# A sparse-attention layer with sorted experts: GpSimd's order, a projection in two halves, the first tiles and the pads

## What is computed

```python
def layer(x, adj):                       # cut from the reference
    n = layernorm(x)
    q, k, v = n @ Wq.T + bq, n @ Wk.T + bk, n @ Wv.T + bv      # 4 heads of 32
    scores = clip(q @ k.T / sqrt(32), -10, 10); scores = where(mask == 0, -10, scores)
    # softmax over EACH chunk of 128 keys by itself; the 8 chunks' contexts are added
    ctx = sum over chunks of softmax(scores[chunk]) @ v[chunk]
    out = ctx @ Wo.T + bo + n
    x = x + layernorm(out) * gamma + beta
    m = layernorm(x)
    two = top2(m @ Wg + bg)
    return x + sum over e in two of (gelu(m @ W1[e] + b1[e]) @ W2[e] + b2[e])
```

## Time and profile before

| | us |
|---|---|
| median of 3 runs | 852.67 |
| lowest, highest | 850.55, 852.83 |
| the profiled execution | 852.1 |
| its span | 850.5 |
| first clip begins, last clip begins | 38.3, 592.1 |
| first finish of a tile, last | 621.9, 839.1 |

### The profile page before, as it was taken

How to read it: one execution, slowest core, us unless ns; L and a number is a source line. 1 busy time by engine, 2 the same in 40 slices (tenths; PEclk the granted TensorE clock), 3 DMA queues, 4 the chain that set the end, 5 groups by cost and what they waited for, 6 DMA issues and landing times. The chain is left out here.

```text
span 850.5 us, 17280 instructions
## 1 busy us (share of the span) xinstructions
PE 722.9 (85%) x5499; PEld 377.7 (44%) x5499; DVE 626.5 (74%) x1472; ACT 491.2 (58%) x873; POOL 591.9 (70%) x674
## 2 busy tenths in 40 slices
PE   2688998998989989899899898787577879999994
PEld 1222233232333333333323333231277768999994
DVE  2178898898988989889898898989774544455552
ACT  2456666766667666676665765635244535666662
POOL 4697665978779787797886977848764556445553
PEclk9989999999999999999999999998787989999998
DMA  7100000011010110101100001003211246432330
GB/s 260 62 1 25 14 13 13 13 39 50 14 39 13 39 50 13 39 13 39 50 13 26 14 27 37 14 26 110 76 54 57 68 133 189 123 85 85 102 93 1
DMA packets 45255, 45.43 MB, mean 53 GB/s; under 512 B 7413, under 2 KB 39424, under 8 KB 44720
## 3 DMA queue, kind: packets, MB, share of 16 engines
q1 hardware_dynamic: 38800, 30.00, 12.6%
q0 software_dynamic: 6368, 14.34, 4.8%
HBM read 31.46 MB, written 18.34 MB: 59 GB/s over the span
## 5 line engine op out<-in xcount | busy, mean ns | idle before, releaser
L641 ACT ACTIVATE e<-e 128x2048 f32<-128x2048 f32 x128 | 244.3, 1910 | 184.1 <-DVE e L783 181.3
L783 DVE SCALAR_TENSOR_TENSOR e<-scores_ps,bound_mem 128x2048 f32<-128x2048 f32 x128 | 291.9, 2281 | 43.8 <-PE scores_ps L393 42.4
L1189 POOL DMA_INDIRECT out<-e,near x91 | 90.3, 993 | 100.2 <-DVE e L964 51.7
L1167 POOL TENSOR_TENSOR ctx_part<-ctx_part,z_inv 128x1024 f32<-128x1024 f32 x62 | 119.8, 1933 | 49.1 <-DVE z_inv L799 49.1
L706 ACT ACTIVATE e<-scores_ps,bound_mem 128x128 f32<-128x128 f32 x364 | 103.8, 368 | 71.0 <-PE scores_ps L532 55.5
L412 PE MATMUL z_ps<-e,one_column 128*32 128x512 f32 x1024 | 137.4, 609 | 0.0
L1179 POOL TENSOR_TENSOR ctx_sum<-ctx_sum,ctx_part 128x512 f32<-128x512 f32 x90 | 115.8, 1287 | 6.0
L532 PE MATMUL scores_ps<-e,bound_mem 128*128 128x128 f32 x728 | 103.3, 287 | 13.7 <-DVE bound_mem L946 7.6
L532 PEld LDWEIGHTS scores_ps<-e,bound_mem 128*128 128x128 f32 x728 | 93.6, 201 | 17.4 <-issue 11.0
L946 DVE COPY bound_mem<-bound_mem 128x258 f32 x182 | 51.3, 324 | 55.6 <-issue 54.9
L791 DVE STREAM_TRANSPOSE ctx_part<-ctx_ps 128x512 f32<-128x512 f32 x128 | 90.1, 704 | 0.1
(11 more groups left out here) (156 smaller groups left out, 1046.7 us busy)
## 6 DMA issues: line engine op xcount, KB each, us to landing
near<-sorted_rows SPq DMA_DIRECT2D x91, 130.0 KB
near<-in_x SPq DMA_DIRECT2D x16, 256.0 KB
bound_mem<-in_adjT SPq DMA_DIRECT2D x4, 1024.0 KB, 11.0
x_post<-in_x SPq DMA_DIRECT2D x16, 256.0 KB, 2.7
sorted_rows<-sorted_rows SPq DMA_DIRECT2D x16, 130.0 KB
sorted_rows<-sorted_rows POOLq DMA_DIRECT2D x12, 130.0 KB
out<-e,near POOLq DMA_INDIRECT x91
sorted_rows<-x_rows,slot POOLq DMA_INDIRECT x64
```

The costliest lines, as they stand in the source:

```text
L641: nc.scalar.activation(every, every, ACT.Exp, scale=SCORE_SCALE).then_inc(exp_done, 1)
L783: dve.scalar_tensor_tensor(out=e[:, s % E_RING], in0=scores_ps[:], scalar=-CLIP, in1=to, op0=ALU.max, op1=ALU.min).then_inc(clipped, 1)
L1167: nc.gpsimd.tensor_tensor(pair, pair, z_inv[:, v % 2, j:j + 2].to_broadcast([P, 2, SQUARES, DH]), ALU.mult).then_inc(ctx_scaled, 1)
L1189: nc.gpsimd.indirect_dma_start(out=out_rows, out_offset=bass.IndirectOffsetOnAxis(ap=near_u[:, id_at:id_at + 1], axis=0), in_=e_flat[:, at ...
```

## The change

1. *GpSimd's order in a block.* Scale, addition, scale now stand ahead of root 2; two additions and a scale ahead of the residual; two additions and a scale ahead of root 3; then two additions. In the last block the scatter of block 12 moves from the end to behind the first scale.
2. *Projection.* `project` takes a range of token tiles; in blocks before the last, four of its eight matmuls stand in step 1 and four in step 2. The rank moves from step 5 to step 6. ScalarE's normalise of the incoming x moves from step 7 to behind the exponential of the next block's step 0.
3. *Hand-over.* The loops end with the last block; the last two contexts, VectorE's turns, the gate and choice of block 13, the projection of block 14 and the sums of block 15 stand in slots 0 to 2 among the tiles. The router's steps get slots with numbers 3 higher or so; the two scales of block 15 go from slot 0 to slots 3 and 4. The read of a tile's offsets (`load_offsets`) moves behind the copy of the tile ahead.
4. *Pads.* SyncE issues 12, two behind each of loads 28 to 33, GpSimd 10 from slot 22, ScalarE 6 from slot 22, one a slot.

```diff
-SP_PADS = 16
-PAD_LOAD, PAD_SLOT = 19, 21
+SP_PADS, POOL_PADS = range(0, 12), range(12, 22)
+ACT_PADS = range(22, NP)
+PAD_LOAD, PAD_SLOT = 28, 22
...
-                if i >= PAD_LOAD and n_padded < SP_PADS:
-                    pad(n_padded)
-                    n_padded += 1
+                for k in SP_PADS[max(2 * (i - PAD_LOAD), 0):max(2 * (i - PAD_LOAD) + 2, 0)]:
+                    pad(k)
...
-                    if j == (2 if last else 1) and is_block(u - 2):
-                        project(u - 2)
+                    if last and j == 2:
+                        project(13)
+                    if not last and j in (1, 2) and is_block(u - 2):
+                        project(u - 2, range(2 * j - 2, 2 * j))
...
                 if k < FFN_TILES:
                     turn_tile(k)
+                if k < LAG:
+                    context(STEPS - LAG + k)
+                if k == 0:
+                    gate(13)
+                if k == 1:
+                    project(14)
...
+            load_offsets(0)
             for k in range(SLOTS):
+                if k < FFN_TILES:
+                    copy_weights(k)
+                if k + 1 < FFN_TILES:
+                    load_offsets(k + 1)
+                if k < LAG:
+                    turn(STEPS - LAG + k)
                 if k == 0:
-                    scale_last(4)
-                    scale_last(6)
...
+                if k in (3, 4):
+                    scale_last(2 * k - 2)
...
+                if k == PAD_SLOT:
+                    act.wait_ge(pad_at_ready, 1)
+                    act.wait_ge(spare_padded, 16)
+                if 0 <= k - PAD_SLOT < len(ACT_PADS):
+                    pad(ACT_PADS[k - PAD_SLOT])
+                if k == 0:
+                    act.wait_ge(z_added, STEPS - 1)
+                if k == E_RING - 1:
+                    act.wait_ge(z_added, STEPS)
```

More of the change, by code:

```diff
@@ L475, in rank, with project @@
                           skip_group_check=True).then_inc(rank_filled, 1)
-            def project(v):
+            def project(v, tiles=range(TILES)):
                 pe.wait_ge(ctxT_ready, v + 1)
@@ L480, in project @@
                 pe.wait_ge(xnT_bo_ready, v + 1)
-                for t in range(TILES):
+                for t in tiles:
                     cols = slice(t * P, (t + 1) * P)
@@ L484, in project @@
                     ins = pe.matmul(job_ps[1][:, cols], xnT_bo[:, v % 4, cols], ident[:], start=False, stop=True)
-                ins.then_inc(proj_filled, 1)
+                if TILES - 1 in tiles:
+                    ins.then_inc(proj_filled, 1)
             def columns(g):
@@ L564, in _ @@
             pe.matmul(job_ps[1][:, 0:1], w_proj[:, W_O, :], bv_sb[:], start=True, stop=True).then_inc(bias_filled, 1)
-            for u in range(FIRST, BLOCKS + 1):
-                for j in range(CHUNKS if u < BLOCKS else LAG):
+            for u in range(FIRST, BLOCKS):
+                for j in range(CHUNKS):
                     s = u * CHUNKS + j
@@ L587, in _ @@
                         queries(u + 2)
-                    if j == (1 if last else 5) and is_block(u - 3):
+                    if j == (1 if last else 6) and is_block(u - 3):
                         rank(u - 3)
@@ L707, in gelus, with pad @@
                                          bias=part_flat[:, bias_at:bias_at + 1]).then_inc(hidden_ready, 1)
+            def pad(k):
+                at = act.value_load(pad_at[0:1, k:k + 1], min_val=0, max_val=SPARE * P)
+                act.dma_start(sorted_rows[bass.ds(at, P), :], sorted_tiles[SPARE]).then_inc(padded_act, 16)
             act.wait_ge(proj_loaded, 16 * 8)
             act.wait_ge(ident_ready, 1)
-            for u in range(FIRST, BLOCKS + 1):
-                for j in range(CHUNKS if u < BLOCKS else LAG):
+            for u in range(FIRST, BLOCKS):
+                for j in range(CHUNKS):
                     s = u * CHUNKS + j
@@ L715, in _ @@
                         exponentials(s)
+                    if j == 0 and is_block(u + 2):
+                        normalise_x(u + 2)
                     if j == 2 and is_block(u + 2):
@@ L932, in _, with load_offsets @@
             offsets_of = {}
[L934 to L937 removed]
+            def load_offsets(i):
                 if i in GROUP_OF:
@@ L1194, in _ @@
             for u in range(FIRST, BLOCKS):
+                last = u == BLOCKS - 1
                 if is_block(u - 1):
                     scale(u - 1, 0)
+                if last:
+                    scatter(u - 3)
+                if is_block(u - 1):
+                    add_context(u - 1, 1)
+                    scale(u - 1, 2)
                 if is_block(u - 2):
@@ L1199, in _ @@
                 if is_block(u - 1):
-                    add_context(u - 1, 1)
-                    scale(u - 1, 2)
                     add_context(u - 1, 2)
+                    add_context(u - 1, 3)
+                    scale(u - 1, 4)
                 if is_block(u - 2):
@@ L1205, in _ @@
                 if is_block(u - 1):
-                    add_context(u - 1, 3)
-                    scale(u - 1, 4)
                     add_context(u - 1, 4)
+                    add_context(u - 1, 5)
+                    scale(u - 1, 6)
                 if is_block(u - 2):
@@ L1211, in _ @@
                 if is_block(u - 1):
-                    add_context(u - 1, 5)
-                    scale(u - 1, 6)
                     add_context(u - 1, 6)
@@ L1226, in _ @@
                     ins.then_inc(gates_spread, 1)
-                if is_block(u - 3):
+                if is_block(u - 3) and not last:
                     scatter(u - 3)
@@ L1237, in _ @@
             for k in range(SLOTS):
[L1238 removed]
+                if k == 7:
                     root(ln["3"], 14)
[L1240 to L1242 removed]
+                if k in (8, 9):
+                    scatter(13, (2 * k - 16, 2 * k - 15))
+                if k == 10:
                     root(ln["2"], 15)
[L1244 removed]
+                if k == 11:
                     add_residual(15)
[L1246 removed]
+                if k == 14:
                     root(ln["3"], 15)
[L1248 to L1251 removed]
+                if k in (15, 16):
+                    scatter(14, (2 * k - 30, 2 * k - 29))
+                if k in (22, 23):
+                    scatter(15, (2 * k - 44, 2 * k - 43))
                 if k == PAD_SLOT:
@@ L1254, in _ @@
                     pool.wait_ge(spare_padded, 16)
-                if 0 <= k - PAD_SLOT < NP - SP_PADS:
-                    pad(SP_PADS + k - PAD_SLOT)
+                if 0 <= k - PAD_SLOT < len(POOL_PADS):
+                    pad(POOL_PADS[k - PAD_SLOT])
                 if k >= 2:
```

120 lines of the change are left out of this document (54 added, 66 removed).

## The result

The kernel after runs in **818.13 us** (median of 4 runs, 817.23 to 819.39), the kernel before beside it in 852.75. The ratio is 0.9596, 95% interval [0.9568, 0.9623]: 34.6 us faster, against a forecast of 823. The profiled execution of after has a span of 816.4 us and a mean granted clock of 0.972.

A forecast was written before the change was run, and what follows sets the result against it. The prediction took the wait cycle between GpSimd's running sum and VectorE to bound attention, and tile loads and stalls the tiles before tile 32. Blocks −20 and hand-over with pads −9 took 852.1 to 823 us; range 806 to 842.

The forecast's parts named there:

- the ring was the bound: Attention blocks: GpSimd's sum, VectorE's turn of it and z_inv wait for each other in a cycle; 823 us, chance 50%.
- part 1: GpSimd's order in the attention blocks: additions and scales cover the root's wait; 1.2 us a block, 13 blocks, 16 us.
- part 3: Hand-over from attention to tiles: tile 0 finished 12.1 us earlier, 5.4 us given back by VectorE's work between tiles.
- part 2: Projection halved over steps 1 and 2 of a block: saves a 0.85 us wait in about every second block, 4 us.
- The last clip: Sign at the end of attention: the last clip ends near 575 us; later than 585 would be wrong.
- keeps its spacing in slots, and so do its stalls: Block 15's router chain among the tiles: its spacing and stalls in slots stay, so the loss up to tile 32 was left.
- Part 4: Pads among the tile loads: 6 us of load waits gone, 1.5 us added at SyncE and 2 at ScalarE.
- a granted clock of 0.5 in more than 10 us of the tiles: Sign in the tile phase that would show the prediction wrong.
- (d): Tile phase: lower clock level gone from the first 20 tiles and stalls halved; 808 us, chance 10%.
- (e): Tile phase: thin start leaves TensorE idle, at the lower clock through the router's slots; slower, 861 us at 20 slots, chance 6%.
- exclusion: Shared SBUF port between tiles: each VectorE scale could wait for a whole GpSimd scale, 3.8 us more; left out.

The follow-up runs named there:

- after's second run: The kernel after, unchanged, run again on another chip than the first: 811.04 us, ratio 0.9622 to the kernel before.
- the later runs: The kernel after, unchanged, run twice more on chips where before takes 842 us: 811.04 and 812.35 us, ratios 0.9622 and 0.9641.

## Why the prediction was right

The chosen case, "the ring was the bound", holds, and 823 lies 5 us above the result. But the terms behind it are not all of the size forecast, and some luck is in the sum: part 1 gives 6 us or more beyond its term, part 3 gives 4 to 7 us where 6.7 was forecast, with a give-back much larger than its term, and part 2 has its size from another wait than the one it prices.

- **Part 1, forecast 16, measured 22 to 24.** The mechanism is as told: the root's wait is covered, the sum comes earlier, the block falls to 33.0 to 33.2 us (forecast 33.4). The term that was mis-sized is the gain per block, 1.2 us over 13 blocks; it is 1.8. It was capped at 1.5 by the time at which TensorE issued the next block's scores. But TensorE itself waited for VectorE's clips, 20.9 us between 130 and 530 us with the old order and 10.3 in after's second run, so its scores come earlier too, and the cap moves. Another 0.3 was taken off for TensorE's turn of xn2. That give-back isn't there: between 130 and 530 us this wait is 6.0 us in 12 places in after and 5.9 in 12 with the old order.
- **Part 2, forecast 4, measured 2.3 to 4.4: the size by luck.** It prices a wait of 0.85 us for the scores of step 2 in about every second block. In before's trace the wait is in 3 of the 12 blocks from 3 to 14, 2.5 us in all, and each time TensorE was granted the lower clock level (1.2 GHz) for some 3.4 us just ahead of it. These three blocks take 35.7 to 35.9 us, the others 34.8, and the block that was read is one of the three. With GpSimd's new order alone, and with the projection whole again, the wait is in none of these blocks, and the granted clock is 1.00. So this part's wait goes with part 1. What the projection's halves and the rank's move give is the 0.23 us a block seen above. The rows are before, just ahead of its wait in block 8, and the kernel with the whole projection:

```profile
314.00:318.00 4.00, 4.00 (x24) 1.14 (x21) 3.90 (x15) 1.23 (x2) 3.36 (x4) 0.57 0.56 168
```

```profile
38.00:560.00 522.00, 480.15 (x3683) 171.00 (x3683) 476.69 (x904) 341.65 (x368) 429.25 (x421) 1.00 0.09 28
```

- **The last clip**, forecast to end near 575, ends at 570.99, by the error in part 1.
- **Part 3, forecast −12.1 and +5.4, and the step that failed.** The start is as forecast: the wait of 1.3 us for tile 0's load measured 1.38, and tile 0 is finished 13.4 us behind the last clip's end (forecast 15, before 27.5), though 15.4 and 17.1 in the later runs. Some 3.9 of this belong to GpSimd's order in the last block, so of the forecast's net of 6.7 about 3 are left for the hand-over itself; it measured 0 to 3. The term that was mis-sized is the give-back: beside the kernel without the hand-over, tile 0 comes 7 to 9 us sooner behind the last clip, as forecast (12.1 less the 3.9), but 8.3 to 10.1 are given back up to tile 32, not 5.4. What the forecast left out stands in its own sentence, that the chain for block 15 "keeps its spacing in slots, and so do its stalls". The forecast made the stalls a property of the slots. They are one of time: z_inv comes 4.7 us later with tile work ahead of it, the tiles start 8 us sooner, and a shift by 3 slots doesn't make up for both. The rows gave z_inv; following the chain from it to ctxT in time, and the tiles beside it, would have shown the stall at slot 8.
- **Part 4, forecast −2.5, measured −4.0 to −5.6.** The forecast took 15.0 us in 12 places as TensorE's waits for loads. That row adds two queues of one engine that stand at the same time, the weight loads (8.2 us in 7 places) and the matmuls. The matmuls alone waited 6.8 us in 5 places, 3.0 of them for the first two tiles:

```profile
PE scores_ps L521 <- DMA near<-sorted_rows: 6.8, 5, 2.3
```

  So the 6 us that the forecast took as gone were more than the 3.8 there. In after these waits are 1.4 us in the first execution (under 6 forecast), 4.9 and 6.5 in the two later ones, of which 3.5 and 5.0 fall at tiles 31 to 33, where none was forecast up to 32. What ScalarE's six pads cost by themselves wasn't measured, and the term was measured with the hand-over in place; without it, projection and pads together give 2.6 us.
- **The clock.** The lowest rows of 10 us in the tiles are 0.67 (600 to 610) and 0.66 (620 to 630), both at a stall of TensorE of over 4 us. At 0.5 or 1.00, the two levels, a row of 0.67 is 6.6 us at the lower one. From 570 to 700 us the mean is 0.88, so about 31 us of 130 were at the lower level: the sign "a granted clock of 0.5 in more than 10 us of the tiles" was there, and it told nothing, since before has the same 0.88 from 594 to 728. Rivals (d) and (e) did not come about: the low level neither went nor spread.
- **The port.** The prediction left out exclusion, 3.8 us by the rule. Alone, VectorE's scale takes 1.22 us, an addition of tile work 0.29, two copies 0.49 and an addition of the sum 0.69; GpSimd's scale takes 1.92 and its next three instructions 1.3 each. Where they meet, one of the two is longer each time:

```profile
585.56 1.22 DVE L829 TENSOR_TENSOR ctx_part<-ctx_part,z_inv 128x1024 f32<-128x1024 f32 x1 [0.43 <-issue]
585.65 2.90 POOL L1199 TENSOR_TENSOR ctx_part<-ctx_part,z_inv 128x1024 f32<-128x1024 f32 x1
586.70 2.00 DVE L979 TENSOR_TENSOR bound_mem<-near 128x128 f32<-128x128 f32 x1
589.01 1.23 DVE L970 COPY bound_mem<-bound_mem 128x258 f32 x2
590.16 2.29 DVE L829 TENSOR_TENSOR ctx_part<-ctx_part,z_inv 128x1024 f32<-128x1024 f32 x1
591.33 2.24 POOL L1191 TENSOR_TENSOR x_post<-x_post,rows 128x512 f32<-128x512 f32 x1
592.37 1.75 DVE L845 TENSOR_TENSOR ctx_sum<-ctx_part 128x512 f32<-128x512 f32 x1
```

That is what the Trainium skill (SBUF — State Buffer, on the shared port pair) lets expect: the addition has two SBUF inputs and is held for most of a GpSimd instruction. VectorE's four longer rows make 4.6 us between 586 and 594, 3.0 of them beyond what the forecast's 5.4 holds, against the 3.8 that it left out. The later runs of after repeat it (4.6 and 4.4 us). How much of it reaches the time of the kernel isn't shown.

The later runs make a chain of kernels, each by its ratio: GpSimd's order, the last block's included, 26.5 us; projection and pads together 2.6 more; the hand-over 1.1 or 2.7. After measured 31.8 and 30.2 by its two ratios. The terms that were measured by taking one part out of after add up to 32 or more (22 to 24, 2.3 to 3.9, 4.0 to 5.6, and the 3.9 of the last block), so they overlap.

## What to carry to other kernels

Where two engines wait for each other in a ring, look for the wait of one that has work of the other's queued behind it: moving ready work ahead of such waits, 3.2 us of it ahead of a 2.5 us wait and more further on, with nothing made faster, gave most of this gain. Starting a phase earlier gives little if steps of the phase before it are tied to slots of the new one: their data keeps its time, so their slots must move later, or they must stand behind the slot's ready work. And a gain at the start of a phase is only counted once a late instant (here the finish of tile 32 and that of tile 89) has been looked at. Before a wait is priced, read it in every block of the trace, not in one, and look at the clock beside it: the 0.85 us of part 2 stood in 3 blocks of 12. And check whether a row of waits adds two queues of one engine.

## What the runs showed of the hardware

The first chip's traces, of before and of after, have places between 634 and 692 us, and a shorter one at 617, where VectorE or ScalarE stands 2 to 5 us and the profile names no instruction on this core as the releaser ("remote"). TensorE stands for 1 to 3 us beside most of them; GpSimd works on in after's. In after:

```profile
DVE e L988 <- remote: 11.3, 3, 4.9
ACT e L716 <- remote: 7.1, 2, 4.6
```

In before VectorE has 6.5 us of these in 2 places and ScalarE 13.3 in 4. None of the twelve traces of the other chips has one, two of them of the same kernel after, so they belong to the chip or the moment, not to the kernels. They are of the size of the difference between the chips (853 and 842 us for before, 818 and 811 to 812 for after), but not all of it: the 57 tiles behind tile 32, where no such place is, take 109.6 us in both traces of the first chip and 107.95 in both later ones of after. In after, two of them (640 to 644 and 664 to 669) lie beside GpSimd's scatters; the other chips have the same scatters without them. What causes them stays open.
